# One pool of six PSUM banks in place of two rings, and a batch normalised one round before its projections

## The reference

```python
mod = (_silu(L0_c) @ L0_wmod).reshape(16, 6, 1, -1)
sa, ca, ga, sb, cb, gb = (mod[:, k] for k in range(6))   # ga, gb: magnitude at least 0.25
h = _layernorm(x) * (1 + ca) + sa
x = x + ga * attention(h)          # 16 heads of 16, causal, a linear bias per head
h = _layernorm(x) * (1 + cb) + sb
x = x + gb * ffn(h)                # 704 hidden, silu(gate) * up
```

## Time and profile before

| | |
|---|---|
| median of 3 runs | 4401.33 us (4390.34 to 4404.51) |
| the profiled execution | 4390.39 us, span 4388.3 us |
| mean granted TensorE clock | 0.967 |
| PE busy | 3890.4 us (89%) |
| DVE busy | 3103.5 us (71%) |
| ACT busy | 2121.6 us (48%) |
| POOL busy | 1186.5 us (27%) |

### The profile page before, as it was taken

How to read it: one execution, slowest core, us unless ns; L and a number is a source line. 1 busy time by engine, 2 the same in 40 slices (tenths; PEclk the granted TensorE clock), 3 DMA queues, 4 the chain that set the end, 5 groups by cost and what they waited for, 6 DMA issues and landing times.

```text
span 4388.3 us, 75144 instructions
## 1 busy us (share of the span) xinstructions
PE 3890.4 (89%) x23668; PEld 2079.9 (47%) x23668; DVE 3103.5 (71%) x5101; ACT 2121.6 (48%) x4175; POOL 1186.5 (27%) x886
## 2 busy tenths in 40 slices
PE   2799989899898998989999898998989899899977
PEld 1335444444454444444544454444544545444445
DVE  6568768587675867768587685867768587686745
ACT  2364545445454454555455454554555455455541
POOL 1413214132231423214132231423213132231213
PEclk6799999999999999999999999999999999999998
DMA  1532122212122132122212122122122212122000
GB/s 57 82 45 43 30 48 40 55 20 40 36 40 55 21 52 38 30 50 40 55 20 40 36 40 55 21 50 38 32 50 39 55 20 40 35 40 45 11 14 10
DMA packets 128139, 171.75 MB, mean 39 GB/s; under 512 B 22020, under 2 KB 75988, under 8 KB 127700
## 3 DMA queue, kind: packets, MB, share of 16 engines
q1 hardware_dynamic: 127700, 166.15, 22.0%
HBM read 47.01 MB, written 16.84 MB: 15 GB/s over the span
## 4 chain that ended last, share of the span: by engine, by line
PE 68%; DVE 15%; ACT 8%; issue 7%; SPq 1%; DMA 1%; POOL 0%; DVEq 0%; ACTq 0%; POOLq 0%
PE o_acc L630 12%; PE a_ring L614 11%; PE d_ring L647 10%; PE d_ring L747 7%; ACT arena L813 7%; PE a_ring L723 7%; PE d_ring L730 5%; PE d_ring L685 3%; PE d_ring L704 2%; DVE top L1032 2%; PE d_ring L650 2%; PE a_ring L617 2%; PE a_ring L677 2%; PE a_ring L739 2%; DVE amaxH L993 2%
## 5 line engine op out<-in xcount | busy, mean ns | idle before, releaser
L813 ACT ACTIVATE arena<-a_ring 128x512 f32<-128x512 f32 (+3 forms) x3072 | 1451.9, 491 | 1243.9 <-PE a_ring L617 924.0
L1032 DVE TENSOR_REDUCE top<-d_ring 128x1 f32<-128x640 f32 (+7 forms) x1408 | 1411.9, 1027 | 498.8 <-PE d_ring L650 468.5
L614 PE MATMUL a_ring<-qa,ka 105*128 105x512 bf16 (+3 forms) x3072 | 999.3, 333 | 182.4 <-ACT arena L813 138.3
L647 PE MATMUL d_ring<-ka,qa 102*128 102x512 bf16 (+3 forms) x3072 | 789.9, 332 | 72.3 <-DVE delta L1134 28.1
L614 PEld LDWEIGHTS a_ring<-qa,ka 105*128 105x128 bf16 x3072 | 294.7, 97 | 953.8 <-ACT arena L813 789.9
L630 PE MATMUL o_acc<-arena,va 128*17 128x512 f32 (+3 forms) x6144 | 644.8, 491 | 1.5 <-ACT arena L813 1.1
L650 PE MATMUL d_ring<-mask,identb 128*128 128x128 bf16 x2048 | 433.4, 224 | 52.4 <-issue 52.4
L941 POOL TENSOR_TENSOR hid<-hid,tm 128x704 f32<-128x704 f32 x128 | 215.3, 1682 | 940.1 <-DVE hid L1004 940.1
L617 PE MATMUL a_ring<-maskT,identb 128*128 128x128 bf16 x2048 | 446.9, 221 | 0.0
L747 PE MATMUL d_ring<-wdT,hqT 128*128 128x256 f32 x1536 | 386.9, 405 | 35.2 <-DVE top L1032 27.0
L647 PEld LDWEIGHTS d_ring<-ka,qa 102*128 102x128 bf16 x3072 | 280.1, 99 | 288.5 <-issue 77.9
(11 more groups left out here) (142 smaller groups left out, 4654.1 us busy)
## 6 DMA issues: line engine op xcount, KB each, us to landing
qa<-parts SPq DMA_DIRECT2D x384, 128.0 KB, 4.5
ka<-parts SPq DMA_DIRECT2D x384, 128.0 KB, 6.3
xa<-in_x SPq DMA_DIRECT2D x16, 1024.0 KB, 6.1
xr<-in_x SPq DMA_DIRECT2D x64, 256.0 KB, 2.7
out_x<-xr SPq DMA_DIRECT2D x64, 256.0 KB, 2.2
ffn_rows<-rows_dram SPq DMA_DIRECT2D x16, 384.0 KB, 3.9
ga_row<-rows_dram SPq DMA_DIRECT2D x16, 128.0 KB, 3.9
qa<-in_w_mod SPq DMA_DIRECT2D x2, 768.0 KB, 5.0
```

The source lines that it names most:

```text
L614: mm = pe.matmul(ps[:, 0:w], ka[g][0:KT, h, kt * P:(kt + 1) * P], qa[g][0:KT, h, q0:q0 + w], start=True, stop=s not in DIAGONAL, skip_grou ...
L647: pe.matmul(ps[:, at:at + z - a], qa[g % NG][0:KS, h0 + m, qt * P:(qt + 1) * P], ka[g % NG][0:KS, h0 + m, a:z], start=True, stop=z < w, sk ...
L813: nc.scalar.activation(probs[:, s % P_SLOTS, h, 0:w], ps[:, 0:w], ACT.Exp).then_inc(a_free, 1)
L1032: nc.vector.tensor_reduce(tops, ps, AX.X, ALU.max).then_inc(d_free, 1)
```

## The change

The two rings become one pool of six banks. The plan gives each event the one or two banks that come free first (a pair starts at an even bank), and it may run up to four events ahead of ACT and two ahead of DVE. Before an event PE waits for whoever last emptied the banks, which can be a count of `a_free`, of `d_free` or both. The planner no longer adds an engine's completion lag to a dependence on the same engine, and some costs are set anew. Loading and normalising (`XA` on SP, `N1`, `N2`, `N3`) are done for batch `b+2` in round `b`, after `SPL(3)` has freed `xa`, with a due time of 0.7 of the round; so `TR` at the start of a round waits for no DVE work, and `TR` and `U` are due earlier. The `start` section normalises batches 0 and 1. The loop has 13 rounds, and a new section `late` stands behind it, in which no batch is normalised.

```diff
+    BANKS, AHEAD = 6, {"A": 4, "D": 2, "Q": 2}
...
+        def place(banks):
+            found = None
+            for n in range(0, self.BANKS, banks):
+                mine = range(n, n + banks)
+                if any(owner[k] and owner[k] not in done for k in mine):
+                    continue
+                t = max(done[owner[k]] if owner[k] else 0.0 for k in mine)
+                pair = owner[n ^ 1]
+                rank = (t, banks == 1 and not (pair and pair not in done), n)
+                if found is None or rank < found:
+                    found = rank
+            return found
...
-                t = max([free[key[0]]] + [done[a] for a in after if a in done])
+                t, where = max([free[key[0]]] + [done[a] for a in after if a in done and a[0] != key[0]]), None
                 if ring:
                     n = len(filled[ring])
-                    if n - emptied[ring] >= 2:
+                    if n - emptied[ring] >= self.AHEAD[ring]:
                         continue
...
+                if banks:
+                    where = place(banks)
+                    if where is None:
+                        continue
+                    t = max(t, where[0])
...
-        p.add("SP", ("XA",), 0.7, 0.0, lag=7.0)
-        for h in range(2):
-            p.add("DVE", ("N1", h), 2.4, 0.05 * L, ("SP", ("XA",)))
+    for k in ([1] if not here and nxt else []) + ([2] if then else []):
+        at = 0.0 if k == 1 else 0.7 * L
+        p.add("SP", ("XA", k), 0.7, at - 10.0, ("POOL", ("SPL", 3)) if k == 2 else None, lag=7.0)
+        for h in range(2):
+            p.add("DVE", ("N1", h, k), 2.4, at, ("SP", ("XA", k)))
...
-                due = (0.12 + 0.12 * u) * L
+                due = (0.04 + 0.04 * u) * L
...
-ROUNDS = B - 2
+ROUNDS = B - 3
...
-        d_ring = ctx.enter_context(nc.psum_tensor("d_ring", [P, 2, 2 * BANK], F32))
-        a_ring = ctx.enter_context(nc.psum_tensor("a_ring", [P, 2, BANK], F32))
+        banks = ctx.enter_context(nc.psum_tensor("banks", [P, Plan.BANKS * BANK], F32))
...
+            def open_banks(e, a=(), d=()):
+                done = max([A.emptied(e)] + [A.number(r) + 1 for r in a])
+                if done > 0:
+                    pe.wait_ge(a_free, A.i * A.per + done)
+                done = max([Dr.emptied(e)] + [Dr.number(r) + 1 for r in d])
+                if done > 0:
+                    pe.wait_ge(d_free, Dr.i * Dr.per + done)
+                return bank(A.section, e)
```

More of the change, by code:

```diff
@@ L70, with add @@
     RINGS = {"A": ("PE", "ACT"), "D": ("PE", "DVE"), "Q": ("DVE", "POOL")}
+    BANKS, AHEAD = 6, {"A": 4, "D": 2, "Q": 2}
     def __init__(self):
         self.jobs, self.order = {}, {e: [] for e in ("PE", "ACT", "DVE", "POOL", "SP")}
[L75 to L77 removed]
+        self.bank, self.before = {}, {}
+    def add(self, engine, event, cost, due, *after, lag=0.06, ring=None, takes=None, lock=None, banks=0):
+        self.jobs[engine, event] = (cost, due, [a for a in after if a], lag, ring, takes, lock, banks)
     def settle(self):
@@ L103, in settle @@
                 if best is None or rank < best[0]:
-                    best = (rank, key, t)
+                    best = (rank, key, t, where)
             assert best, sorted(left)[:20]
-            _, key, t = best
-            cost, due, after, lag, ring, takes, lock = left.pop(key)
+            _, key, t, where = best
+            cost, due, after, lag, ring, takes, lock, banks = left.pop(key)
             engine, event = key
@@ L115, in settle @@
                     held = None if lock[1] else lock[0]
+            if banks:
+                first = where[2]
+                self.bank[event] = (first, banks)
+                self.before[event] = [owner[k] for k in range(first, first + banks)]
+                owner[first:first + banks] = [(self.RINGS[ring][1], event)] * banks
             if takes:
@@ L278, in index, with emptied @@
         return self.i * self.per + self.number(event)
-    def slot(self, event):
-        return self.number(event) % 2
+    def emptied(self, event):
+        counts = [0]
+        first, banks = PLANS[self.section].bank[event]
+        for k, owner in enumerate(PLANS[self.section].before[event], first):
+            if owner and owner[1] in self.place:
+                counts.append(self.number(owner[1]) + 1)
+            elif not owner and self.section == "start":
+                counts.append(len(SETUP_A if self.name == "A" else SETUP_D))
+            elif not owner:
+                for s in FOLLOWS[self.section]:
+                    last = PLANS[s].owner[k]
+                    if last is None:
+                        counts.append(self.base)
+                    elif last[1] in self.places[s]:
+                        counts.append(self.base - len(self.jobs[s]) + self.places[s][last[1]] + 1)
+        return max(counts)
 STEP_COST = {"O": 2, "LR": 11, "XA": 2, "XR": 3, "XQ": 3, "HR": 3, "HQ": 3, "N1": 2, "N2": 11, "SM": 3, "ON": 1}
```

145 lines of the change are left out of this document (73 added, 72 removed).

## The result

The median is 4481.44 us (4 runs, 4475.66 to 4488.57) against 4402.3 us of the kernel before beside it: a ratio of 1.0182, 95% interval 1.0163 to 1.0202. The change costs 1.8%. The forecast, 4156 us, has the wrong sign, and the range (4010 to 4430) doesn't hold the time.

What follows compares the result with a forecast made beforehand. The prediction took ring A's two slots to cost 22 us a round. Its sum: 4390.4 profiled - 240 (four T ahead) - 45 (normalisation) + 48 (new waits) + 3 (start section) = 4156 us, range 4010 to 4430.

Steps and rivals of the forecast that it cites:

- What bounds the kernel: Attention steps: ring A's two slots limit, not PE or ACT; 0.45 us lost per us of load wait, 22 us a round.
- Four T ahead of ACT: Attention in 16 rounds: two thirds of the 22 us saved, 15 us a round, -240 us; dropped lag counted here.
- The step of the earlier trace: Stretch with T and PV alone: PV to PV was to fall from 2.94 us to 2.1 to 2.3 us.
- The change doesn't do what it says: Rival: the plan seldom finds a third free bank, A stays at two, 4377 to 4415 us; chance 0.09.
- New waits: T in a bank that DVE empties: one wait of 3 us a round, +48 us in 16 rounds.
- Shared banks tie T to DVE: Rival: 64 T a round take DVE's banks, each waiting 0.35 us; 4486 us at 6 us a round; chance 0.15.
- The clock rival: Short, frequent PE idling keeps the clock at 0.83 over 210 us of PE work a round: 4844 us; chance 0.02.
- Normalisation moved: Round start, before the feed-forward net: PE waits less for DVE, 3 us in 15 rounds, -45 us; bounds 0 and 6.6.
- TR, U and SPL earlier: POOL's splitting beside DVE work: the collision moves and does not go, 0, bounds 2.5 us a round either way.
- The seam: Loop's jump back: PE's 3.8 us wait for nothing visible stays, as many seams as before; 0 in the sum.
- What would show it wrong: Signs: PE waits for DVE beyond 8 us a round, T loads wait for DVE, clock falls, load waits above 40 us.

Runs made afterwards that it cites:

- pure_pool: The kernel before with only the six-bank pool and ring A four ahead; lag rule, costs, normalisation and due times stay old: 4386.05 us (0.9968).
- ahead_two: The changed kernel with A two ahead in place of four, in the same pool of six banks: 4308.3 us (0.9791).
- unrolled: The changed kernel with its 13 loop rounds written out, order of work unchanged: 4353.57 us (0.9906).
- two_unrolled: The changed kernel with A two ahead in place of four and its loop rounds written out: 4185.18 us (0.9512).
- lag_alone: The kernel before with only the new lag rule and the new costs: 4390.85 us (0.9986).
- norm_old_dues: The kernel before with only the normalisation moved; TR and U keep their old due times: 4306.19 us (0.9791).
- norm_unrolled: The kernel before with only the normalisation moved, TR and U at their old due times, and its loop rounds written out: 4215.41 us (0.958).
- rings_again: The changed kernel with the banks dealt out as the two rings of before, two ahead each: 4436.96 us (1.0092).
- norm_alone: The kernel before with only the moved normalisation and the earlier due times of TR and U: 4498.36 us (1.0241).

## Why the prediction was wrong

**What bounds the kernel.** That the two slots of ring A cost 22 us a round is the first error. The rate of 0.45 us lost per us of load wait came from one step without other work and was spread over all load waits of a round. pure_pool removed 334 us of these waits for 15 to 33 us of time, 0.04 to 0.10 per us, and at most 0.20 if its longer waits for DVE are added back. That this is because `T` has `S` and the feed-forward net around it in most places is likely, and no run separates it.

**Four T ahead of ACT, -240 us. The step that failed.** The load waits halved as named, but two ahead in the pool nearly halves them as well (789.9 in before, 412.3 in ahead_two, 396.1 in after), and allowing four costs 168 us (unrolled against two_unrolled) instead of gaining 240. The step of the earlier trace rows that should fall to 2.1 to 2.3 us takes 2.87, and ACT's idle time before the exponentials rose from 70.9 + 16.9 to 77.6 + 22.6 us a round. The banks were counted rightly ("a depth of four holds only while DVE holds one event"), and then two thirds of the gain were taken all the same: DVE does hold more, half of the `T` keep two slots, and the price of the order that comes with the depth was not in the sum. Here the rival "The change doesn't do what it says" had half of the mechanism. The dropped lag, counted in this term, is worth nothing alone (lag_alone).

**New waits, +48 us, and the rival.** The sign was right; PE's waits for DVE grew by 80 us over the run (141.8 to 221.5). The rival "Shared banks tie T to DVE" gave 4486 us, 5 us from the median, but not by its own mechanism, so its closeness is chance: it wanted more than 51 waits of 0.35 us a round. What came is few and long, in the round shown four load waits and two of PE, up to 3.3 us, with DVE waits of `S` beside them, and a low clock behind them. The clock rival was right that waits would cost clock, but it wanted short and frequent idling and a low clock all through the round. The clock falls at the jump and in two places of a round. Its 210 us of PE work a round come from no row either: windows over a round of before have PE busy for about 90% of it.

**Normalisation moved, -45 us.** Right in sign, and in the mechanism for half of it, and too small: 94 us in norm_old_dues (88 without jumps), 6 us a round and near the upper bound of 6.6. In norm_unrolled PE's waits for DVE fell by 43.7 of these 88 us, and its busy time by 40.7. Of the busy time the mean clock (0.973 to 0.976) makes only some 12 us, an estimate: 3864.4 x (1 - 0.973/0.976); the rest isn't explained. In the trace of after `N1` begins at 1579.95, behind the load that SP issues at 1570.71, and does not wait for it.

**TR, U and SPL earlier, 0 with 2.5 us either way.** The bound was too narrow: 192 us or 12.8 us in each of 15 rounds on the rings, 45 us or 3 us the other way in after. The collision was named rightly; its price isn't fixed by the edit but by where the order puts it.

**The seam, 0. Failed.** "As many seams as before" says nothing of what one costs. It went from 7.4 to 10.7 us, 32 us in all, and what fits is that `DN(7)`, short and behind a wait for ACT, now ends the section and not `V(1)`. The pairs with rounds written out agree: a jump costs 7.4 and 7.6 us where `V(1)` is last (before, norm_old_dues), 10.7 and 10.3 where `DN(7)` is (after, ahead_two). It isn't all: by PE's waits alone a jump shows 6.9 us in pure_pool, with `V(1)` last, and 5.8 in rings_again, with `DN(7)`.

**What would show it wrong** came: PE's waits for DVE are above 8 us a round, loads of `T` wait for DVE rows, and the clock falls inside a round.

**The sum.** Without jumps, before to after is +50 us: the depth of four +168, everything else together -118. The move of the normalisation makes 88 of these on the rings. How the other 30 divide among pool, lag, costs and dues stays open, since these do not add. The +168 belongs to this base: pure_pool allows four as well and is no slower than before, and no run gives it two. Why the order for four makes DVE come late stays open too, beyond what the planner's reckoning shows. No kernel tried the depth of three.

The best version is two_unrolled: the change with two ahead and its rounds written out, 4185.18 us, 4.9% below before. With the loop kept, ahead_two and norm_old_dues are 2.1% below.

## What to carry to other kernels

Waits of weight loads tell where a buffer is short, not what it costs: price them by a run that removes them, not by the one stretch where nothing covers them. Where engines share buffers in a written order, try the pool with the smallest depth first, and count in the order how many buffers each event really has before counting on the depth. Look at what stands last before a loop's jump, since it can cover part of the jump; and try a moved step apart from the new due times that come with it.

## What the runs showed of the hardware

- The jump back of a loop costs PE 7.4 to 10.7 us here, of which its waits without a visible cause show (52.4 + 12.1) / 13 = 5.0 and 109.9 / 12 = 9.2. The first load comes 5.7 us after the last matmul, and a second gap of 3.4 us follows after one load. The Trainium skill, Runtime: NRT & Kernel Launch, section Instruction fetch mechanics, says that a taken branch out of the fetched window stops the engine until the target is fetched, and that kernels are better written out. That the gaps vanish in unrolled agrees with it.
- A small DVE instruction that meets POOL waits for the rest of POOL's instruction as a large one does: line 1050 with its 32 columns takes 1.31 us in the timeline above. Its mean over 64 is 0.45 us in norm_alone and 0.20 in norm_old_dues.
